# VectorE's step operations with one input in SBUF: reciprocals, ranks, indices and weights in spare PSUM columns

## What is computed

```
tokens = einsum('bnpd,edp->bne', patches(x, 16, stride 8), W) + b     # 64 x 93 x 128
h = tokens + attn(layernorm(tokens))
h = h + ffn(layernorm(h))

attn: xn = layernorm(x)*gamma + beta
      q, k, v = three-tap causal convolutions of wq1@xn, wk1@xn, wv1@xn   # 8 heads of 64
      attn = softmax(q k^T * scale + alibi bias, causal)                  # 93 x 93
      out = (attn v) @ wout.T
ffn:  top_vals, top_idx = top_k(x @ gate.T, 2)          # of 16 experts
      routing_w = softmax(top_vals)
      h_mean[e] = mean over expert e's rows of silu(w1[e] x)
      y_mean[e] = w2[e] h_mean[e]
      out = sum_k routing_w[k] * y_mean[top_idx[k]]
```

## Time and profile before

| | |
|---|---|
| median of 3 runs | 791.71 us (791.15 to 791.81) |
| the profiled execution | 791.94 us, span 790.3 us |
| PE busy | 706.6 us, 89% |
| DVE busy | 605.4 us, 77% |
| ACT busy | 607.5 us, 77% |
| POOL busy | 382.8 us, 48% |
| chain that ended last, by engine | PE 36%, DVE 34%, ACT 18%, issue 8% |
| granted TensorE clock, mean | 0.971 |

### The profile page before, as it was taken

One profiled execution on the slowest core, in us unless ns is written; L12 is line 12 of the kernel. 1 busy time (PEld: TensorE's weight loads), 2 busy tenths in 40 slices (PEclk: granted clock), 3 DMA queues, 4 the chain that ended last, 5 costly groups with the idle time before them and its releaser, 6 DMA issues.

```text
span 790.3 us, 21100 instructions
## 1 busy us (share of the span) xinstructions
PE 706.6 (89%) x6514; PEld 626.4 (79%) x6514; DVE 605.4 (77%) x1579; ACT 607.5 (77%) x2022; POOL 382.8 (48%) x390
## 2 busy tenths in 40 slices
PE   4789999989998999999898989888888778999986
PEld 4678898878787888888797878776677577999983
DVE  2167778887888888888888798887887558888865
ACT  3557898978887888888787978787886757899960
POOL 3642434756556465565565656554362565122200
PEclk9889999999999999999999999999998969999996
DMA  5522124322211121211212122102124112122205
GB/s 181 146 79 60 48 87 145 103 78 61 59 51 50 48 54 45 53 49 49 64 40 64 49 52 55 47 12 68 26 78 164 32 48 68 52 69 63 63 19 156
DMA packets 44273, 53.99 MB, mean 68 GB/s; under 512 B 13651, under 2 KB 31251, under 8 KB 43696
## 3 DMA queue, kind: packets, MB, share of 16 engines
q1 hardware_dynamic: 30048, 38.84, 17.2%
q0 software_dynamic: 12544, 12.87, 6.1%
q10 hardware_dynamic: 1616, 1.48, 0.6%
HBM read 42.69 MB, written 10.26 MB: 67 GB/s over the span
## 4 chain that ended last, share of the span: by engine, by line
PE 36%; DVE 34%; ACT 18%; issue 8%; DMA 2%; POOL 1%; SPq 1%; DVEq 0%; ACTq 0%
ACT prob L805 12%; DVE qkv L979 6%; DVE qkv L982 5%; DVE prob L1095 4%; PE psSO L707 4%; PE psTP L707 4%; PE psTP L451 4%; DVE rmin L1065 4%; PE psTP L453 3%; PE psTP L452 3%; DVE sel L1161 3%; PE psSO L652 3%; PE psTP L523 3%; ACT qkv L785 3%; PE psSO L542 3%
## 5 line engine op out<-in xcount | busy, mean ns | idle before, releaser
L1326 POOL DMA_INDIRECT expert_rows<-hn,slot x128 | 174.7, 1365 | 74.8 <-DVE slot L1174 44.8
L805 ACT ACTIVATE prob<-psSO,rmin 93x93 f32<-93x93 f32 x512 | 151.8, 354 | 20.8 <-DVE rmin L1065 20.8
L1259 POOL TENSOR_TENSOR x_lo<-x_raw,x_hi 128x752 fp32r<-128x752 f32 x64 | 115.0, 1797 | 52.5 <-ACT x_hi L777 52.0
L785 ACT ACTIVATE qkv<-psTP,taps 128x372 f32<-128x372 f32 x192 | 112.5, 586 | 21.8 <-PE psTP L453 21.1
L979 DVE SCALAR_TENSOR_TENSOR qkv<-psTP,taps,qkv 128x368 f32<-128x368 f32 x192 | 112.6, 586 | 20.3 <-ACT qkv L785 20.3
L982 DVE SCALAR_TENSOR_TENSOR qkv<-psTP,taps,qkv 128x364 f32<-128x364 f32 x192 | 114.5, 596 | 6.8
L451 PE MATMUL psTP<-x_hi,wtok_hi 128*128 128x376 f32 x256 | 98.9, 386 | 11.1 <-DVE wtok_lo L967 9.1
L805 ACT ACTIVATION_READ_ACCUMULATOR prob<-psSO,rmin 93x1 f32 x512 | 98.2, 192 | 0.0
L451 PE MATMUL psTP<-xnT_hi,wqkv_hi 128*128 128x372 f32 x192 | 80.3, 418 | 17.8 <-DVE qkv L982 17.7
L453 PE MATMUL psTP<-x_hi,wtok_lo 128*128 128x376 f32 x256 | 87.6, 342 | 0.0
L452 PE MATMUL psTP<-x_lo,wtok_hi 128*128 128x376 f32 x256 | 87.5, 342 | 0.0
(11 more groups left out here) (194 smaller groups left out, 1730.2 us busy)
## 6 DMA issues: line engine op xcount, KB each, us to landing
x_raw<-in_x SPq DMA_DIRECT2D x64, 376.0 KB, 3.2
w1s<-in_w POOLq DMA_DIRECT2D x8, 512.0 KB, 4.9
w<-in_w SPq DMA_DIRECT2D x4, 1024.0 KB, 6.0
out<-resid SPq DMA_DIRECT2D x16, 160.0 KB, 2.7
xsE<-expert_rows SPq DMA_DIRECT2D x36, 64.0 KB, 2.1
xs<-expert_rows SPq DMA_DIRECT2D x36, 64.0 KB, 1.8
xs<-expert_rows POOLq DMA_DIRECT2D x36, 64.0 KB, 2.1
expert_rows<-hn,slot POOLq DMA_INDIRECT x128, 3.5
```

Source lines behind the costliest of these rows:

```text
L785: nc.scalar.activation(qkv[u][:, k, :, :], psP[(k + 1) % 2][:, 0:GT].rearrange("p (b n) -> p b n", n=NT), ACT.Copy, scale=taps[:, k, 2:3]) ...
L805: i = nc.scalar.activation(prob[:, a, hh, :], psS[:NT, a, hh * NT:(hh + 1) * NT], ACT.Exp, bias=rmin[:, a, hh:hh + 1], scale=-1.0, accum_o ...
L1259: nc.gpsimd.tensor_tensor(x_lo[u][:, 0:PIECE], x_raw[u][:, :], x_hi[u][:, 0:PIECE].bitcast(F32), ALU.subtract)\
L1326: nc.gpsimd.indirect_dma_start(rows, bass.IndirectOffsetOnAxis(slot[1 - u][:, c:c + 1], 0), hn[1 - u][:, c % GB, :], None)\
```

## The change

Six tiles leave SBUF for columns of PSUM banks that are in use already, at columns that nothing else holds at that time: `den` and `rden` (columns 372 to 379 of the two score banks), and `idxf`, `wden`, `wts`, `slotf` (columns 384 to 411 of the fourth bank of `psSO`, which the gate's logits use earlier in the step). `pos` is written over `psRank`. Where an operation had two SBUF inputs that lie in one tile, it becomes a reduction over pairs of one input: `gap` (now first minus second, so its exponential takes a scale of -1), `mask` and `rw`. `prob` times `rden`, `sel`, `hot`, `wsel` and the second weight keep one input in SBUF and take the other from PSUM. Two waits of PE change: a piece's scores wait for the multiplied `prob` of the piece before instead of its reciprocals, and the transposes of `hn` in part 2 also wait for `rw`. The number of instructions and their order are the same on every engine.

```
-        rden = sb("rden", [NT, 2, 4])
-        idxf = sb("idxf", [NT, 2, GB])
-        wts = sb("wts", [NT, 2, GB])
-        wden = sb("wden", [NT, GB])
-        pos = sb("pos", [NT, GB * E])
-        slotf = sb("slotf", [NT, 2 * GB])
+        idxf = psO[:NT, 1, 384:392].rearrange("p (k b) -> p k b", k=2)
+        wden = psO[:NT, 1, 392:396]
+        wts = psO[:NT, 1, 396:404].rearrange("p (k b) -> p k b", k=2)
+        slotf = psO[:NT, 1, 404:412]
+        den, rden = psS[:NT, :, 4 * NT:4 * NT + 4], psS[:NT, :, 4 * NT + 4:4 * NT + 8]
...
                 wait(pe, exp_done, n * 2)
-                wait(pe, rden_done, n)
+                wait(pe, prob_ready, n)
...
                         wait(pe, base_done, t - 4)
+                        wait(pe, rw_done, t - 4)
...
-                        nc.scalar.activation(egap[:, :], gap[:, :], ACT.Exp).then_inc(egap_done, 1)
+                        nc.scalar.activation(egap[:, :], gap[:, :], ACT.Exp, scale=-1.0).then_inc(egap_done, 1)
...
-                        nc.vector.reciprocal(rden[:, :, :], psS[:NT, :, 4 * NT:4 * NT + 4]).then_inc(rden_done, 1)
+                        nc.vector.reciprocal(rden, den).then_inc(rden_done, 1)
...
                         nc.vector.tensor_tensor(prob[:, :, :, :], prob[:, :, :, :],
-                                                rden[:, :, :].unsqueeze(3).broadcast_to([NT, 2, 4, NT]),
+                                                rden.unsqueeze(3).broadcast_to([NT, 2, 4, NT]),
                                                 ALU.mult).then_inc(prob_ready, 1)
...
-                nc.vector.tensor_tensor(gap[:, :], top[:, :, 1], top[:, :, 0], ALU.subtract).then_inc(gap_done, 1)
+                nc.vector.tensor_reduce(gap[:, :], top[:, :, 0:2], AXX, ALU.subtract).then_inc(gap_done, 1)
...
-                nc.vector.tensor_tensor(mask[:, :].rearrange("p (b e) -> p b e", e=E), hot[:, 0:GB, :],
-                                        hot[:, GB:, :], ALU.add).then_inc(mask_done, 1)
+                    nc.vector.tensor_reduce(mask[:, :], hot[:, :, :].rearrange("p (k b) e -> p (b e) k", k=2), AXX, ALU.add)\
+                        .then_inc(mask_done, 1)
...
-                nc.vector.tensor_tensor(pos[:, :].rearrange("p (b e) -> p b e", e=E),
+                nc.vector.tensor_tensor(psRank.rearrange("p (b e) -> p b e", e=E),
...
                 nc.vector.tensor_tensor(sel[:, :, :].rearrange("p (k b) e -> p k (b e)", k=2),
                                         hot[:, :, :].rearrange("p (k b) e -> p k (b e)", k=2),
-                                        pos[:, :].unsqueeze(1).broadcast_to([NT, 2, GB * E]), ALU.mult)\
+                                        psRank.unsqueeze(1).broadcast_to([NT, 2, GB * E]), ALU.mult)\
...
-                nc.vector.tensor_tensor(rw[:, :, 0:E], wsel[:, 0:GB, :], wsel[:, GB:, :], ALU.add).then_inc(rw_done, 1)
+                nc.vector.tensor_reduce(rw[:, :, 0:E], wsel[:, :, :].rearrange("p (k b) e -> p b e k", k=2), AXX, ALU.add)\
+                    .then_inc(rw_done, 1)
```

More of the change, by code:

```diff
@@ L806, in exponentials @@
                                              bias=rmin[:, a, hh:hh + 1], scale=-1.0,
-                                             accum_out=psS[:NT, a, 4 * NT + hh:4 * NT + hh + 1])
+                                             accum_out=den[:, a, hh:hh + 1])
                 i.then_inc(exp_done, 1)
@@ L1129, in route @@
                 i.then_inc(topi_done, 1)
-                nc.vector.tensor_tensor(gap[:, :], top[:, :, 1], top[:, :, 0], ALU.subtract).then_inc(gap_done, 1)
+                nc.vector.tensor_reduce(gap[:, :], top[:, :, 0:2], AXX, ALU.subtract).then_inc(gap_done, 1)
             def choose(g):
                 wait(dve, topi_done, g + 1)
-                nc.vector.tensor_copy(idxf[:, :, :], topi[:, :, 0:2].rearrange("p b k -> p k b")).then_inc(idxf_done, 1)
+                nc.vector.tensor_copy(idxf, topi[:, :, 0:2].rearrange("p b k -> p k b")).then_inc(idxf_done, 1)
                 wait(dve, idxf_done, g + 1)
                 nc.vector.tensor_tensor(hot[:, :, :], iota.unsqueeze(1).broadcast_to([NT, 2 * GB, E]),
-                                        idxf[:, :, :].rearrange("p k b -> p (k b)").unsqueeze(2)
+                                        idxf.rearrange("p k b -> p (k b)").unsqueeze(2)
                                         .broadcast_to([NT, 2 * GB, E]), ALU.is_equal).then_inc(hot_done, 1)
                 wait(dve, hot_done, g + 1)
-                nc.vector.tensor_tensor(mask[:, :].rearrange("p (b e) -> p b e", e=E), hot[:, 0:GB, :],
-                                        hot[:, GB:, :], ALU.add).then_inc(mask_done, 1)
+                with nc.allow_low_precision(reason="sums of zeros and ones"):
+                    nc.vector.tensor_reduce(mask[:, :], hot[:, :, :].rearrange("p (k b) e -> p (b e) k", k=2), AXX, ALU.add)\
+                        .then_inc(mask_done, 1)
             def rank(g, u):
@@ L1156, in place @@
                 wait(dve, egap_done, g + 1)
-                nc.vector.tensor_scalar(wden[:, :], egap[:, :], 1.0, None, ALU.add).then_inc(wden_done, 1)
+                nc.vector.tensor_scalar(wden, egap[:, :], 1.0, None, ALU.add).then_inc(wden_done, 1)
                 wait(dve, wden_done, g + 1)
-                nc.vector.reciprocal(wts[:, 0, :], wden[:, :]).then_inc(w0_done, 1)
+                nc.vector.reciprocal(wts[:, 0, :], wden).then_inc(w0_done, 1)
                 wait(dve, pos_done, g + 1)
@@ L1167, in place @@
                 wait(dve, sel_done, g + 1)
-                nc.vector.tensor_reduce(slotf[:, :], sel[:, :, :], AXX, ALU.add).then_inc(slotf_done, 1)
+                nc.vector.tensor_reduce(slotf, sel[:, :, :], AXX, ALU.add).then_inc(slotf_done, 1)
                 wait(dve, w1_done, g + 1)
                 nc.vector.tensor_tensor(wsel[:, :, :], hot[:, :, :],
-                                        wts[:, :, :].rearrange("p k b -> p (k b)").unsqueeze(2)
+                                        wts.rearrange("p k b -> p (k b)").unsqueeze(2)
                                         .broadcast_to([NT, 2 * GB, E]), ALU.mult).then_inc(wsel_done, 1)
                 wait(dve, slotf_done, g + 1)
-                nc.vector.tensor_copy(slot[u][:, :], slotf[:, :]).then_inc(slot_done, 1)
+                nc.vector.tensor_copy(slot[u][:, :], slotf).then_inc(slot_done, 1)
                 wait(dve, wsel_done, g + 1)
                 wait(dve, rwT_evac, g)
-                nc.vector.tensor_tensor(rw[:, :, 0:E], wsel[:, 0:GB, :], wsel[:, GB:, :], ALU.add).then_inc(rw_done, 1)
+                nc.vector.tensor_reduce(rw[:, :, 0:E], wsel[:, :, :].rearrange("p (k b) e -> p b e k", k=2), AXX, ALU.add)\
+                    .then_inc(rw_done, 1)
                 wait(dve, base_done, g + 1)
```

## The result

The changed kernel takes 767.83 us (median of 4, 767.50 to 768.34) where the kernel before takes 791.76 in the same comparison: the ratio is 0.9676, interval 0.9655 to 0.9697. It is 3.2% faster. The forecast was 772.5 with a range of 768 to 784, so the time lies just outside, at the fast end: 19.2 us were expected, 23.9 came. The profiled executions are 791.94 and 768.05 us, 23.9 apart as well.

The account below looks back on a forecast made before the run. PE's work, 34.8 us of a 37.1 us step, was the floor. Steady steps -18.3, other terms -0.9, -1.6, -0.5, +1.9, +0.2: together -19.2 from 791.94, hence 772.5 us by the median; range 768 to 784.

Parts of the forecast that it names:

- the three lines named: DVE's `sel`, `gap` and part 2 `prob`, held beside `x_lo`, lose 2.43, 0.66 and about 0.8 us a steady step.
- the 2.33 us: PE's standing time in a steady step of 37.1 us, taken as the most a faster DVE can give.
- 9 x (2.33-0.3): Nine steady steps each lose PE's standing time except 0.3 us: -18.3 us.
- The 0.3 us that I left standing: PE's remaining wait in a steady step: 0.1 for PSUM operands on the part 1 path, 0.2 for small misfits.
- The reading of the held lines: DVE lines reading two SBUF tensors stand beside POOL's `x_lo`; lines with one SBUF input never stand.
- The witness step: The step from 131.2 us, `sel` free at 255 ns: 35.87 us, without part 0's 1.0 us wait, 1.25 us standing left.
- The first rival: Only `sel` pays, the waits behind part 3 stay: 10 steps give 1.0 us each, 784 us; chance 0.20.
- Operands in PSUM: DVE's reciprocal and product take 0.1 us more together with PSUM operands; a `sel`-like operation nears 20 ns more.
- The rival of slow broadcasts: DVE fetches `rden` from PSUM at half rate for each of 744 elements, 0.78 us a product: 797 us; chance 0.05.
- The rival that the locks stay: DVE is held for working in SBUF at all while GpSimd reads it; nothing goes: 794 us; chance 0.05.
- The scores' new wait: Scores wait for the product: little lost in steps with convolutions, +1.9 us over three last pieces, 0.8 at the first piece.
- nothing left standing: No PE standing left in a step: 769 us, or 768 if the last pieces cost nothing more.

Follow-up runs that it names:

- all but `sel`: The changed kernel with `pos` back in SBUF, so that `sel` alone has two SBUF inputs; 780.91 us, ratio 0.9855.
- both ends in SBUF: The changed kernel with the reciprocals in SBUF and the old wait for the first two pieces and from piece 52 on; 765.75 us, ratio 0.9633.
- all but `prob`: The changed kernel with the reciprocals in SBUF and the old wait of the scores in every piece; 774.76 us, ratio 0.9759.

## Why the prediction was right, and where it was wrong

**What bounds the kernel.** Right in the main: PE is the floor, DVE's held instructions were what kept the kernel from it, and the three lines named are the ones. In the changed kernel PE is busy for 34.08 us of a 34.33 us step, and 0.5 us more of DVE's work in part 0 does not lengthen it.

**The step that failed** is the sentence that what a faster DVE can give in a step is at most the 2.33 us, and with it the term 9 x (2.33-0.3). PE's idle time is not what PE's stops cost. The timeline of PE around the stop in part 0 shows the rest, the kernel before first:

```profile
393.29 0.33 PE L452 MATMUL psTP<-x_lo,wtok_hi 128*128 128x376 f32 x1
393.46 0.33 PE L453 MATMUL psTP<-x_hi,wtok_lo 128*128 128x376 f32 x1
394.90 0.44 PE L451 MATMUL psTP<-xnT_hi,wqkv_hi 128*128 128x372 f32 x1 [1.10 <-DVE qkv L982]
395.18 0.33 PE L452 MATMUL psTP<-xnT_lo,wqkv_hi 128*128 128x372 f32 x1
```

and the same place in the changed kernel:

```profile
339.33 0.33 PE L451 MATMUL psTP<-x_lo,wtok_hi 128*128 128x376 f32 x1
339.50 0.33 PE L452 MATMUL psTP<-x_hi,wtok_lo 128*128 128x376 f32 x1
339.67 0.33 PE L450 MATMUL psTP<-xnT_hi,wqkv_hi 128*128 128x372 f32 x1
339.84 0.33 PE L451 MATMUL psTP<-xnT_lo,wqkv_hi 128*128 128x372 f32 x1
```

Matmuls start 0.17 us apart and last 0.33: two are always under way. At the stop the last matmul before it counts as busy for 0.16 us in which nothing new is started, and the first one behind it takes 0.44 and is followed 0.28 later, not 0.17. From start to start this stop took 1.27+0.11 = 1.38 us more (393.46 to 395.18 is 1.72, 339.50 to 339.84 is 0.34), while the view of waits says 1.10. PE's busy time fell by 0.7 us a step. One stop brought back, in the kernel with all but `sel`, raised it by 0.29; that the other stops that went hid the remaining 0.4 is inferred from the sum. So a step gave 2.8 us, 2.1 of idle and 0.7 of busy time, and 9 x 2.8 = 25.2 in place of the term's 18.3. The 0.3 us that I left standing came out by luck, at 0.25: it was meant for PSUM operands and misfits, and what is left is the stop of 0.3 behind a convolution at the transposes of the tokens (L601), which I had counted among those that go.

**The reading of the held lines** was too narrow. I wrote that lines with one SBUF input never stand, from the three lines in the earlier trace rows. `wden` has one, and stood 2.8 us once. The forecast did not suffer, since the change moved that line too, but the rule of two inputs would have missed it elsewhere.

**The witness step** was read too narrowly. It did show what goes with `sel`, the 1.0 us wait. And it had the missing part in it: it is 1.26 us shorter than a steady step (35.87 against 37.13) for an absent wait of 1.0. It was no witness for freeing `sel` alone: there nothing was held in `place` at all, while a kernel with only `sel` freed has its weight held instead and gains 0.3%. The first rival, that only `sel` pays, was priced at 1.0 a step as well, where the kernel with all but `sel` shows 1.36. It did not come up: the other waits went too.

**Operands in PSUM.** I took 0.1 us for reciprocal and product together; it was 0.01. `sel` shows nothing for its PSUM input: 253 ns with it against 255 in the kernel before, and 270 in the changed kernel against 270 without it in the kernel with all but `sel`. The Trainium skill (VectorE: DVE Perf Modes, the section on the TRN2 errata) gives a PSUM source 62 cycles more than one in SBUF, an estimate of 65 ns at its 0.96 GHz; no row of this case shows them. The rival of slow broadcasts fell with it: 744 elements from eight PSUM columns at 925 ns. The rival that the locks stay fell too, though the ground given against it, that nothing with one SBUF input is held, was not true of `wden`.

**The scores' new wait.** Right that it is free in the steady steps (37.1 to 37.25 us with and without it in the kernel before), and right in size where it isn't: in the kernel with the old `gap` the clock stayed at 1.00 through the last pieces, and there the three intervals between products were 6.76, 7.12 and 6.80 us where they had been 6.12, 6.16 and 6.44, 1.96 us more against a forecast of 1.9. What I left out is the clock. In the changed kernel the stops of PE ahead of those scores are these:

```profile
589.89 0.49 PE L536 MATMUL psSO<-bias,ident 93*93 93x372 bf16 x2 [1.31 <-DVE prob L1095]
597.06 0.49 PE L536 MATMUL psSO<-bias,ident 93*93 93x372 bf16 x2 [1.09 <-DVE prob L1095]
```

and from 593.00 to 607.17 us the granted clock is 0.66, where before the change the stretch from 622.00 to 632.33 had 0.96:

```profile
593.00:607.17 14.17, 11.22 (x98) 9.60 (x94) 6.60 (x30) 8.75 (x40) 4.07 (x4) 0.66 0.07 16
```

```profile
622.00:632.33 10.33, 6.44 (x78) 5.34 (x77) 6.72 (x30) 6.77 (x32) 4.35 (x3) 0.96 0.09 19
```

With it the intervals were 6.75, 7.17 and 8.56: 1.8 us more than the wait alone. The clock differs from kernel to kernel there: both traces of the changed kernel had 0.83 over the last pieces, the one with the old `gap` 1.00, the one with both ends in SBUF, so without the new wait, 0.85 and still 24.4 us. With only `sel` freed, the old wait too, it cost time:

```profile
609.41:616.43 7.02, 6.07 (x57) 4.39 (x56) 3.42 (x13) 4.20 (x22) 2.85 (x6) 0.84 0.19 67
```

where the kernel before has 6.12 us at 1.00. So of the 3.8 us the new wait made 2.0, and 1.8 went with the lower clock. Whether the stops at the new wait brought that clock on stays open. The 1.3 us of the last `place` and the second phase are of the size by which that part differs between traces (135.4 to 140.7 us for the second phase).

**The two steps ahead of the last pieces** were put at nothing, without a reason, and took 0.9 us more. PE stands there for the product eight times, 5.7 us together, but that is not shown to be the cause: the kernel with all but `prob`, which has the old wait, took 66.62 us there against 66.84, and the one with only the new wait 66.49.

**The range** ended at 768 because I took the fastest case to be nothing left standing by idle time. It ought to have taken a stop from start to start. By the forecast's own terms its end was rounded up: 772.5, less ten times 0.3 and less 1.9 at the last pieces, is 767.6. That the time came so near to the range is in part luck, since the forecast had the start and the steps 8.6 us too long and the end 3.9 us too short.

Two things stay open. That it is `x_lo` that holds rests on the times at which the held instructions end; no kernel took the split away from GpSimd. And the scores' new wait comes with the reciprocals' place: by the Trainium skill (PSUM — Partial Sum Buffer, the section on bank collisions) TensorE may not write a bank while VectorE reads it, whichever columns they touch, and `rden` lies in the banks of the scores. No run here shows that, and the old wait with the reciprocals in those banks was not tried.

## What to carry to other kernels

When a tiny VectorE instruction has a long median or maximum and a short minimum, look for a GpSimd instruction that ends with it, and count the inputs in SBUF of both. One SBUF input is no proof of safety: `wden`, SBUF to SBUF, was held as long as `sel`. Free all such instructions that follow each other in the stretch, since the hold passes to the next one. Price a stop of TensorE from matmul start to matmul start, not by the idle time in the profile, which missed a fifth of one here. And where operands are moved to PSUM, keep the old form in the parts of the pipeline where nothing is held: there the move only brings its wait, and the version with both ends in SBUF took 765.75 us where the changed kernel took 768.87 beside it.

## What was unexpected of the hardware

- A DVE instruction with two SBUF inputs was held from before `x_lo` started: `sel` at 464.33 with `x_lo` from 465.11, the weight at 426.56 with `x_lo` from 427.13, both while a scatter was still running on GpSimd. With a scatter followed by another scatter it wasn't held (`sel` at 575.24, 0.26 us). Two copies of one SBUF input to SBUF were held while scatters ran all the same: `idxf` (L1135) 412 ns from 626.52, to the end of a scatter at 626.96, where 154 is the median, and a copy of `w1s` (L371) 910 ns from 662.85, where 415 is the least. The queued `x_lo` seems to have its claim already; that was not tested by itself.
- Writing small DVE results to PSUM cost at most 13 ns (reciprocals 203 to 212 and 173 to 186 ns; `wden` 156 to 150), and a broadcast from PSUM ran at the pace of one from SBUF.
